# The second feed-forward of a macaron block, sorted by expert for six of its eight chunks

## The reference, cut to what matters

```
x = x + 0.5 * ffn(layernorm(x))          # first feed-forward
x = x + attention(layernorm(x))          # q, k, v; causal softmax; projection; + resid; norm; gamma, beta
x = x + 0.5 * ffn(layernorm(x))          # second feed-forward: the one changed

def ffn(x):                              # x: 4 x 1024 rows of 256
    gamma = softmax(x @ w_router.T + b_router)          # 8 experts
    mask = the two experts with the largest gamma
    y_all = x @ w_experts[e].T + b_experts[e], for all e
    return sum over e of mask[e] * y_all[e]
```

## Time and profile before

| | us |
|---|---|
| median of three runs | 983.08 (982.25 to 985.8) |
| span of the profiled execution | 980.6 |
| the median less that span | 2.5 |
| first feed-forward with q, k, v | 0 to about 315 |
| attention | about 315 to 750 |
| second feed-forward, after the attention's last product | 750.4 to 980.6 |

### The profile page before, as it was taken

The page is one execution under the profiler, slowest core; times in us unless marked ns, Lnnn a source line. Parts: engine busy times, 40 slices in busy tenths (PEclk is TensorE's granted clock), DMA queues, the critical chain, the costliest instruction groups (busy, mean ns, idle before and its releaser), DMA issues.

```text
span 980.6 us, 17661 instructions
## 1 busy us (share of the span) xinstructions
PE 948.2 (97%) x5602; PEld 564.8 (58%) x5602; DVE 824.3 (84%) x2445; ACT 511.1 (52%) x1053; POOL 259.5 (26%) x286
## 2 busy tenths in 40 slices
PE   6999999999999999999999999999988999999998
PEld 5778887776776333333333333333344777787776
DVE  5876777787697999999999999999767888888765
ACT  5325424414316677777777777777775334333210
POOL 1112214202203222222222212222343554434310
PEclk9999999999999999999999999999999999999999
DMA  6301121101114322333322222223320122110001
GB/s 224 96 1 65 65 66 65 65 1 65 54 44 132 99 78 78 79 78 79 76 76 66 71 64 66 65 70 79 98 58 13 44 66 65 64 64 22 1 22 43
DMA packets 55121, 64.37 MB, mean 66 GB/s; under 512 B 13830, under 2 KB 37366, under 8 KB 55030
## 3 DMA queue, kind: packets, MB, share of 16 engines
q1 hardware_dynamic: 54444, 62.52, 22.2%
q10 hardware_dynamic: 592, 0.80, 0.2%
HBM read 41.30 MB, written 21.23 MB: 64 GB/s over the span
## 4 chain that ended last, share of the span: by engine, by line
PE 87%; DVE 6%; ACT 3%; issue 2%; DMA 1%; SPq 1%; POOL 1%; DVEq 0%; ACTq 0%; POOLq 0%
PE bank L368 40%; PE bank L1654 14%; PE bank L1475 13%; PE bank L1636 13%; PE bank L873 3%; PE bank L360 2%; DVE bank L1502 1%; ACT b_probs L1610 1%; DMA v_all<-L_ffn_w_experts 1%; PE bank L815 1%; DVE a_acc L1109 1%; DVE b_neg L1506 0%; PE bank L802 0%; DVE a_st L320 0%; DVE a_rest L1120 0%
## 5 line engine op out<-in xcount | busy, mean ns | idle before, releaser
L1610 ACT ACTIVATE b_probs<-bank 128x512 f32<-128x512 f32 (+1 forms) x608 | 302.7, 585 | 111.0 <-PE bank L1636 110.4
L1502 DVE CUSTOM_DVE_ANT_0 bank<-bank,b_below 128x384 f32<-128x384 f32 (+3 forms) x512 | 235.5, 516 | 7.9 <-PE bank L1475 6.4
L1475 PE MATMUL bank<-b_ks,b_qs 96*128 96x512 bf16 (+3 forms) x768 | 220.8, 328 | 9.0 <-issue 5.1
L1636 PE MATMUL bank<-b_qs,b_ks 99*128 99x512 bf16 (+3 forms) x768 | 213.0, 328 | 4.8 <-ACT b_probs L1610 4.7
L368 PE MATMUL bank<-we,a_xt 128*128 128x512 f32 x768 | 192.6, 402 | 1.6 <-DVE a_acc L1109 1.2
L368 PE MATMUL bank<-we,c_xt 128*128 128x512 f32 x768 | 186.1, 398 | 0.4 <-DVE c_acc L1109 0.4
L1581 POOL TENSOR_SCALAR_AFFINE_SELECT b_probs<-b_probs 128x512 f32<-128x512 f32 x128 | 84.6, 661 | 310.7 <-ACT b_probs L1610 310.5
L1506 DVE TENSOR_REDUCE b_neg<-bank 128x1 f32<-128x512 f32 x256 | 161.2, 680 | 2.6 <-PE bank L1475 1.2
L368 PEld LDWEIGHTS bank<-we,c_xt 128*128 128x128 f32 x768 | 142.3, 188 | 32.2 <-DVE c_acc L1109 0.6
L368 PEld LDWEIGHTS bank<-we,a_xt 128*128 128x128 f32 x768 | 140.9, 189 | 29.8 <-DVE a_acc L1109 1.9
L1654 PE MATMUL bank<-b_probs,b_vs 128*32 128x512 f32 (+3 forms) x1536 | 155.1, 498 | 1.6 <-POOL b_probs L1581 1.6
(11 more groups left out here) (142 smaller groups left out, 905.9 us busy)
## 6 DMA issues: line engine op xcount, KB each, us to landing
b_qs<-q_parts SPq DMA_DIRECT2D x96, 128.0 KB, 3.0
b_ks<-k_parts SPq DMA_DIRECT2D x96, 128.0 KB, 3.0
q_parts<-a_part SPq DMA_DIRECT2D x16, 384.0 KB, 2.6
k_parts<-a_part SPq DMA_DIRECT2D x16, 384.0 KB, 2.7
att_num<-b_oev SPq DMA_DIRECT2D x64, 64.0 KB, 2.2
c_num<-att_num SPq DMA_DIRECT2D x8, 512.0 KB
c_rec<-att_rec SPq DMA_DIRECT2D x16, 256.0 KB
out<-xs SPq DMA_DIRECT2D x7, 512.0 KB, 3.2
```

The costliest lines, as they stand in the source:

```text
L1475: last = nc.tensor.matmul(ms[bank][:, a * width:(a + 1) * width], qs[g.u][0:ROWS, c, i * P:(i + 1) * P], ks[g.u][0:ROWS, c, lo:lo + width] ...
L1502: last = dve.tensor_tensor_reduce(part, part, below[:, CH - width:CH], -1.0, 3.0e38, ALU.add, ALU.min, dst[:, a, :])
L1610: act.activation(probs[b % 4][:, heads[0]:heads[0] + hp, 0:width], es[exp_bank(g, unit)][:, 0:hp * width].rearrange("p (h w) -> p h w", w= ...
L1636: last = nc.tensor.matmul(es[exp_bank(g, unit)][:, a * width:(a + 1) * width], ks[g.u][:, c, j * P:(j + 1) * P], qs[g.u][:, c, first_q:fir ...
```

## The change

In the second feed-forward, chunks 1 to 6 are no longer multiplied by all eight experts. They form three groups of two chunks (1024 rows, 2048 pairs of a row and one of its experts). `ffn(first=False)` is replaced by a new function, `closing`. For each group:

1. `count` and `counted`: after the ranks, TensorE multiplies the 0/1 masks with a triangular matrix and with ones (bf16), which gives for every row and expert how many rows before it chose that expert; VectorE copies that out.
2. `places`: a chain of eleven small VectorE operations rounds each expert's count up to tiles of 128, and gives each pair a place among 23 tiles (SLOTS), and each tile its expert's column in the weights.
3. `scatter`: GpSimd writes the normalised rows to memory at their places with 16 indirect DMAs (8 tiles, two places each). Unused places hold what was there, at first zeros that SyncE wrote in the first feed-forward (2 x 3 MB).
4. `load_rows`, `rows_turn`, `rows_hi`, `rows_lo`: SyncE loads two tiles of places at a time, TensorE transposes them, ScalarE and VectorE split them.
5. `rows_expert`: for each tile TensorE loads the expert's column into a register and does six matmuls of 256 columns, and one of bf16 for the bias.
6. `rows_out`, `store_rows`: ScalarE halves the product and SyncE stores it in memory.
7. `add_results`: when the whole group is stored, GpSimd gathers with 8 indirect DMAs that add the first expert's results into `xs`, waits for them, and gathers with 8 more for the second; `store_group` stores both chunks.

Chunks 0 and 7 stay dense; their expert bias now comes from a seventh matmul of each bank (ones times `bias_all`), the projection's bias from one more matmul for each tile, the router's from VectorE. Beta is added by GpSimd (`shift`), gamma by VectorE (`affine`). The router of chunks 1 to 6 multiplies in fp32 with the rows as the stationary operand. The order on TensorE is written out by hand: chunk 0, with projections 2 to 4 and the routers of 1 to 3 in between; the group loop; chunk 7. The chunks 3 to 7 are fed within the loop over the 12 pairs of tiles of group 0.

```
+SORTED = ((1, 2), (3, 4), (5, 6))
+SLOTS = 2 * 2 * TPC + NE - 1
+PAIRS = (SLOTS + 1) // 2
+ROWS_IN = 6
-        back = ffn(nc, s, ctx, middle, False)
+        back = closing(nc, s, ctx, middle)
...
# front, SyncE
-            sp.dma_start(s.bproj[:], s.b_proj).then_inc(q.later_in, 16)
+            sp.dma_start(s.bias_parts.rearrange("n (e d) -> e n d", e=NE), be_part[:]).then_inc(q.later_in, 16)
+            sp.wait_ge(q.bproj_step, 4)
+            sp.wait_ge(q.ones_ready, 4)
+            sp.dma_start(s.bproj_b[0:3, :], bp_part[:]).then_inc(q.later_in, 16)
+            for places in s.row_places:
+                sp.dma_start(places.rearrange("(p k) (a d) -> p (k a) d", p=P, d=P),
+                             s.zeros[:].unsqueeze(1).broadcast_to([P, SLOTS * D // P, P])).then_inc(q.later_in, 16)
...
# front, GpSimd, between the memset of bias_rows and the affine_select of before
+            pool.memset(s.ones_b[:], 1.0).then_inc(q.ones_ready, 1)
+            pool.memset(s.bproj_b[:], 0.0).then_inc(q.ones_ready, 1)
+            pool.memset(s.zeros[:], 0.0).then_inc(q.ones_ready, 1)
+            pool.iota(grid[:], pattern=[[1, SLOTS + 1]], base=0, channel_multiplier=0).then_inc(q.ones_ready, 1)
...
# front, VectorE
             ranks(0, 0)
+            projection_bias_parts()
             norm(1)
...
# closing, GpSimd
+        def scatter(g):
+            pool.wait_ge(placed, at(g + 1))
+            pool.wait_ge(row_turned, at(PAIRS * (g - 1)))
+            if g:
+                pool.wait_ge(scattered, 16 * 4 * TPC * g)
+            for i, m in enumerate(SORTED[g]):
+                pool.wait_ge(xh_ready, at(m + 1))
+                for t in range(TPC):
+                    for n in range(2):
+                        k = TPC * i + t
+                        pool.indirect_dma_start(
+                            s.row_places[g % 2], bass.IndirectOffsetOnAxis(ap=place_of[g][:, n, k:k + 1], axis=0),
+                            xh[m % 4][:, t, :], None).then_inc(scattered, 16)
+        def gather(g, n, done):
+            for k in range(2 * TPC):
+                pool.indirect_dma_start(
+                    s.xs[:, TPC * SORTED[g][0] + k, :], None, s.y_places[g],
+                    bass.IndirectOffsetOnAxis(ap=place_of[g][:, n, k:k + 1], axis=0),
+                    compute_op=ALU.add).then_inc(done, 16)
+        def add_results(g):
+            for slot in range(4):
+                pool.wait_ge(row_stored[slot], at(16 * len(range(slot, PAIRS * (g + 1), 4))))
+            gather(g, 0, added_a)
+            pool.wait_ge(added_a, 16 * 2 * TPC * (g + 1))
+            if g:
+                pool.wait_ge(added_b, 16 * 2 * TPC * g)
+            gather(g, 1, added_b)
...
+        shift(3)
+        add_tiles(0, range(TPC))
+        scatter(0)
+        shift(4)
+        shift(5)
+        scatter(1)
+        shift(6)
+        shift(7)
+        add_results(0)
+        scatter(2)
+        add_results(1)
+        add_results(2)
...
# closing, ScalarE, in the loop over n = 12 g + j
+            if (g, j) == (0, 11):
+                spread(6)
+                norm(6)
+                turned_out(6)
+                spread3(7)
+                norm3(7)
+                spread(7)
+                norm(7)
+                split_hi(7)
...
# closing, TensorE
+        def rows_expert(n):
+            g, j = divmod(n, PAIRS)
+            if j == 0:
+                pe.wait_ge(placed, at(g + 1))
+            pe.wait_ge(row_lo, at(n + 1))
+            pe.wait_ge(row_out, at(n - 1))
+            for k in range(width(j)):
+                first = pe.value_load(column[g][0:1, 2 * j + k:2 * j + k + 1], min_val=0, max_val=(NE - 1) * D)
+                out_ = ring[2 + n % 2][:, k * D:(k + 1) * D]
+                steps = [(x, w, h) for h in range(DK) for x, w in ((0, 0), (0, 1), (1, 0))]
+                for i, (x, w, h) in enumerate(steps):
+                    nc.tensor.matmul(out_, row_t[n % 3][x][:, k, h * P:(h + 1) * P], s.we[w][:, h, ds(first, D)],
+                                     start=(i == 0), stop=False)
+                last = nc.tensor.matmul(out_, s.ones_b[:], bias_all[:, ds(first, D)], start=False, stop=True)
+            last.then_inc(row_done, 1)
...
+        turn(1, 2)
+        experts(0, 0)
+        project(2, 2)
+        router(1)
+        experts(0, 1)
+        project(3, 2)
+        experts(0, 2)
+        turn(2, 4)
+        count(1)
+        experts(0, 3, (0, 1))
+        router(2)
+        experts(0, 3, (2, 3))
+        project(4, 3)
+        count(2)
+        turn(3, 5)
+        router(3)
+        for n in range(PAIRS * len(SORTED)):
+            g, j = divmod(n, PAIRS)
+            if j == 0:
+                rows_turn(n)
+                rows_turn(n + 1)
+            rows_expert(n)
+            if j + 2 < PAIRS:
+                rows_turn(n + 2)
...
+            if (g, j) == (0, 11):
+                count(5)
+                turn(6, 7)
+                project(7, 7)
+                router(6)
+                count(6)
+                turn(7, 8)
+                router(7)
+        for t in range(TPC):
+            experts(NCH - 1, t, rows_before=PAIRS * len(SORTED))
...
# closing, VectorE, in the same loop
+            if (g, j) == (0, 11):
+                counted(5)
+                add_both(7)
+                stats3(7)
+                scale3(7)
+                ranks(6)
+                counted(6)
+                places(2)
+                affine(7)
+                norm(7)
+                scale(7)
+                split_lo(7)
+                ranks(7)
```

687 lines of the change are left out of this document (681 added, 6 removed).

## The result

The changed kernel takes 1069.87 us (median of 4 runs, 1067.56 to 1073.51) against 983.32 for the kernel before on the same chip: ratio 1.0881, 95% interval 1.0853 to 1.091. It is 8.8% slower; the forecast was 5.0%, 1032 us, within a range to 1090. Its profiled span is 1067.0 us.

What follows compares the result with a forecast made beforehand. TensorE's own work was taken as the bound. Attention's end at 751.4, places 808.4, rows 834.6, group 0 922.6, groups 1 and 2 992.8, GpSimd's tail 1027.2, with clock 1029, plus 2.5 gave 1032 us; range 990 to 1090.

Steps and rivals of the forecast that it cites:

- GpSimd becomes the bound: Rival, chance 0.17: at 2.2 us per indirect DMA GpSimd's scatters and gathers set the time, 1070 us.
- chain at pair 11: Last pair of group 0: feeding chunks 6 and 7 through three engines takes 37 us, TensorE working 13.
- TensorE's work: All TensorE work after attention, summed part by part: about 183 us, 43 less than before the change.
- Hand-over (a): End of attention: TensorE idles 3.6 us for chunk 1's normalised rows, which its first transpose now needs.
- the front: Kernel start: VectorE's four bias operations precede chunk 1's normalisation and delay a combine TensorE awaits, +1.0 us.
- Before the first group (b): Ahead of group 0: places at 808.4, 16 scatters at 1.3 us each, rows at 834.6; TensorE idle some 23 us.
- Group 0 (c): First sorted group: pairs 25.9 us, feeds 15.8 and the last pair's chain 37.1, together 79 us.
- Clock (e): After TensorE's long stalls: the clock drops for a while, two stalls over 20 us costing 2 us or so.
- The address (d): Each sorted tile: loading its expert column into a TensorE register costs 0.4 us, 27.6 us over 69 tiles.
- The rival at 1.4 us: Rival, chance 0.13: the register load holds TensorE 1.4 us per sorted tile, uncovered; 1101 us.
- Everything small is cheap: Rival, chance 0.12: 0.4 us per indirect DMA and no address cost; 986 us, up to 1010 with one priced in between.
- faster: Rival, chance 0.08: small costs cheap and idle in the last pair's chain under 16 us; 962 at none.

Runs made afterwards that it cites:

- the four edits: Changed kernel with chunks 6 and 7's feed spread over group 1, and one beta addition, column loads and next group's first row loads moved earlier; 1050.7 us.
- the spread feed: Changed kernel with the block feeding chunks 6 and 7 moved from group 0's last pair to pairs 0 to 10 of group 1; 1053.45 us.
- the two kernels built on them: On the four edits: plain gathers with VectorE adding, 1029.77 us; on that kernel, the places of group 0 computed sooner, 1027.69 us.

## Why the prediction was right, and by how much it was off

The direction and the reason were right: TensorE was the bound, the saved matmuls are fewer than the stalls that the sorting brings, and the time is in the range. The mechanism was right in each of the stalls named; sizes were off, and one kind of stall was missing. The time is not in the likeliest band, 1010 to 1055, and that it equals the 1070 of the rival "GpSimd becomes the bound" is chance: that rival had 2.2 us per indirect DMA and the first rows at 849, and measured were 1.27 and 1.85, and 836. The signs set beforehand came: rows at 836 (not before 820), pairs of 2.8 us for 3.0, 26 us of idle at pair 11 for 24, the chain ending in the gathers of group 2. Term by term, forecast and measured, in us:

| term | forecast | measured | off |
|---|---|---|---|
| attention's last product | 751.4 | 753.2 | +1.8 |
| to the places | 57.0 | 57.7 | +0.7 |
| scatter, landing, load | 26.2 | 25.3 | -0.9 |
| group 0, tiles, feeds, address | 50.9 | 63.8 | +12.9 |
| chain at pair 11 | 37.1 | 44.3 | +7.2 |
| group 1, to the rows of group 2 | 35.1 | 40.8 | +5.7 |
| group 2 | 35.1 | 39.4 | +4.3 |
| dense chunk 7 | 26.6 | 26.0 | -0.6 |
| from TensorE's end to the span's | 7.8 | 16.5 | +8.7 |
| clock, as a term of its own | 2 | in the above | -2 |

The sum of the last column is 37.8, the distance from 1029.2 to the span of 1067.0.

*TensorE's work.* It was forecast at 183 us after attention and is 211.0 busy, so this term was too small by 28. With a fixed column it is 200.6, so some 10 us of busy time come with the register load, which the forecast had as a separate term; part of the rest is the clock, below, and what is left is open. One sum in it is wrong: eight periods of 29.15 make 233 us and not 226; the 226 is right as the distance from 750.4 to the last combine, and close to the 224.8 busy of the window.

*Hand-over (a).* 3.70 us, as forecast (3.6). Attention ended later than the front explains: the combine that TensorE waits for in the earlier trace rows came 1.04 us later, 26.00 against 24.96, as priced, and another 1.8 us arose by the end of the attention. The changed kernels here end their attention between 752.0 and 755.5; what moves it is open, and it adds up to 3.5 us of noise to a comparison of two spans.

*Before the first group (b), and the price of an indirect DMA.* The estimate of 1.3 us was 1.27 for a scatter: between SyncE's 0.40 and the landing of 2.2 in the earlier trace rows the middle held. That was luck, since no row spoke for the middle. The same price was used for the gathers, and there it was wrong, 1.85. The plain gathers show that the addition inside the DMA is the difference. In the tail it is 16 x 0.55 = 8.8 us, the whole of the 8.7. "GpSimd becomes the bound" decides from 1.9 us: it did not come about in the middle of the changed kernel (one gather stretch less moved group 2 by 0.4 us), but did at group 2 once the feed was spread, and it sets the end in the changed kernel too (11 us less without the second gathers). The Trainium skill ("SBUF — State Buffer", SBUF: two separate sides), on which that rival leaned, has VectorE keeping GpSimd from writing descriptors, 3100 ns instead of 620. The longest of the 96 in the changed kernel was 1.75 us busy, and the longest in any run 2.51 (the four edits): no run here shows 3100 ns.

*Group 0 (c).* This term failed. I added tiles and feeds end to end with no wait between engines, 50.9 us; it took 63.8, with 17.9 us of idle time in five waits. The largest, 7.03, is the consequence of (b) that I did not follow: GpSimd's queue holds two additions behind its 16 scatters, and VectorE and ScalarE hang on the first. The prediction names what is queued behind a waiting instruction at pair 11, but not here. Moving one of the additions brought the first product 5.1 us forward.

*The chain at pair 11.* TensorE's idle time in it was 26.2 us (7.33, 1.22, 4.47, 10.67, 2.50) against 24 forecast; its work was 17.8 against 13, at a clock of 0.58. The order of the steps was read rightly; what a product costs just after a stall was not.

*Clock (e).* This was another mis-sized term, 2 us. The earlier trace rows showed 1.25 us lost behind a stall of 1.8. Here the windows show 0.50, the 1.2 GHz level, from 812 to 836, of which TensorE was busy for 5.5 us, 0.58 through the chain and 0.88 in groups 1 and 2, each of which begins after a stall: six row products take 1.65 us at 948 and 988, and 0.96 later. Not every gap did this: after 1.70 us of idle, at 872.47, six products took 0.97 us, after 3.25, at 878.52, 1.64. The two routers behind stalls, 3.59 and 5.28 us at 815 and 939 against 1.85 and 2.84 for the same calls at 855 here and at 939.79 in the four edits without indirect DMA, lose 4.2 us alone, more than the whole term. Between the changed kernel and that with four edits and no indirect DMA, which issues the same products, on zeros, busy time falls by 14.3 us while the clock rises from 0.80 to 0.88. That is not all the clock's: with only the column loads moved, busy time fell by 3.6 us (to 207.4) at a clock of 0.79. No run changed the clock alone, so its share stays open.

*The address (d).* 0.34 us per tile measured in group 1, 0.50 in group 2, 0.1 in group 0, 0.25 over the whole time (17.5 us of 69 tiles); 0.4 taken. The rival at 1.4 us is out, and so is full cover by the tile before. The Trainium skill ("DMA: Bandwidth & Descriptors", Latency and other measured facts) would have it at about 600 ns; the measurement decides: 0.34 to 0.50 us is what is left uncovered where no other wait covers it.

*Groups 1 and 2.* The 36.7 for 35.1 of group 1 holds two errors that nearly cancel: the tiles took 32.6 (2.8 us a pair for 3.05), and ahead of them stand 4.1 us from the first transposes to the first product, which the forecast had at nothing. In group 2 the second error stays (3.3 us) and the first is gone, because the load costs more there. The 4.0 us ahead of group 2 was missing: its loads stand behind group 1's last store in SyncE's queue.

*"Everything small is cheap"* and *faster*: with every indirect DMA free the time is still 1037.7, and with the chain taken apart too 1012.3, both above the 986 of that rival. The rival's bottom was too low, since the waits replace one another: the spread feed cleared 33.6 us at group 1 and kept 16.

## What to carry to other kernels

Saving an engine's work is worth nothing until the waits that come with it are summed, and the sum has to include what is queued behind each waiting instruction on every engine, above all the small elementwise jobs of the engine that gets the long new work. When one stall is removed, expect the next queue to take part of the gain: here 34 us became 16, in part because the edit itself put a norm ahead of an output, and four edits together gave no more than one until GpSimd's gathers were made cheaper. In a kernel whose TensorE has run without gaps, count each new gap with the slower products after it.

## What the runs showed that I had not expected

- An indirect DMA of 128 rows of 1 KB occupies GpSimd for 0.96 us and 0.30 to the next as a scatter, 0.95 and 0.30 as a plain gather, and 1.54 and 0.30 when it adds. Three plain ones cost about two that add.
- A VectorE operation on 128 x 4 elements took 4.41 us while GpSimd made two additions of 1024 columns, against 0.16 alone; 4.84, 4.83 and 4.83 in the four edits and the two kernels built on them. It ended with GpSimd's second addition (896.2). A VectorE addition of 1024 columns took 3.25 instead of 1.23 and ended 1.1 us after GpSimd's second (837.8 and 836.7).
- A column read from SBUF into a TensorE register costs 0.34 us per tile of seven matmuls in group 1, whether it stands between the tiles or ahead of the pair, and 0.50 in group 2.
